# Biases as a 97th row of the weights, one instruction a bank, residual in place, loops written out: a ViT tower kernel

## The chip, the cores and the metric

The kernel runs on one core of one Trainium2 chip. The metric is the device time of one execution in microseconds. Engines are named as in the profile: PE is TensorE (PEld its weight loads), DVE is VectorE, ACT is ScalarE, POOL is GpSimd, SP is SyncE, which here only issues DMAs.

## The reference

Sixteen images of 3 x 64 x 64 are tokenised into 256 tokens of 192 features; then one attention block and one tree-routed feed-forward layer, each with a residual. What the change touches is the attention:

```python
h = tokens(x)                                            # (16, 256, 192)
qkv = layernorm(h) @ W_attn + b_attn                     # 12 heads of 16
scores = q @ k.T / 4, causal; attn = softmax(scores)
h = h + (attn @ v) @ W_proj + b_proj
h = h + fff(layernorm(h), weights_in, weights_out)       # 21 nodes, 11 levels
```

All of it is float32. b_attn and b_proj are not zero.

## The kernel before

There are five hand-written instruction streams, one for each engine, that meet at semaphores. Constants: `B` = 16 images, `S` = 256 tokens (`TT` = 2 tiles of `P` = 128), `D` = 192 features in two halves of `HALF` = 96, `H` = 12 heads, `G` = 3 groups of four heads.

The work has three stages. First the tokens: POOL issues 42 indirect gathers, PE, DVE and ACT turn them into `HT`, the residual stream (128 x 32 tiles x 192, kept in SBUF). Second, sixteen steps, one an image. Third, the second layernorm, the logits, the walk through the tree, and the output.

A step is software-pipelined by hand over four images. `step(b)` on each engine takes the scores and maxima of image b, the last third of the exponentials and the weighted sum of image b-1, the output projection of image b-2, the q, k and v projections of image b+1, and the normalised, transposed tokens of image b+2. Steps 0, 1, 14 and 15 are written out; steps 2 to 13 are a hardware loop (`Fori`) of six trips of two steps on PE, DVE, ACT and POOL. SP's are written out.

What the change and the prediction touch, in the order of PE's stream in a step:

- `qk(b+1, w)`, L1020: for w = 0 (q) and 1 (k) eight float32 matmul instructions of 256 columns (two for each call in the code) into bank `MB`: weights `WA`, moving `XNT`. Then for each w: `first_part` on ACT (L423) rounds the bank plus bias `BQK` to bfloat16 in `PART[0]`; `rest` on DVE (L686) computes bank + bias - `PART[0]` into `RES`; `middle` on ACT (L430) rounds `RES` into `PART[1]`; `low` on POOL (L312) subtracts the two into `PART[2]`. `first_part` and `rest` take two instructions each, since the per-partition bias differs between the two halves of the bank. SP copies the three parts, six 96 x 512 DMAs for q and six for k, into `QS` and `KS` (L251), where six products of parts are stacked on 96 rows.
- `scores(b, u)`, L1047/L1048 and L1052/L1053, u = 0 to 8: scores and mask into two banks; DVE takes their row maxima (L676, L678).
- `minus_max(b, g)` on DVE: two small instructions of 128 x 8, L714 (tensor_scalar) and L716 (scalar_tensor_tensor), write the negated maxima in two bfloat16 parts into `MP`; `max_t(b, g)`, L1073, transposes them on PE; ACT copies them to `MT` (L456); SP copies `MT` into two more rows of `QS` (L258).
- `scores_t(b, v)`, L1090 and L1094: the transposed scores minus maxima; ACT takes the exponentials (L450); POOL cuts them causally (`causal`: L323, L327); `weighted(b, g)`, L1109 and L1112, sums the values.
- `project(b-2)`, L1141; `residual` on DVE (L722) adds bank and `HT` into `H2`; `residual_bias` adds `BP` in place (L728), takes statistics (L732), copies `H2` back into `HT` (L734), aggregates (L736) and copies mean and variance into `MV` (L738).
- `v_proj(b+1)`, L1031, then `values` on DVE: two instructions (L695) add `BV` and write `VA`.
- `on_t(b-1)`, L1132, and `outputs_t` on ACT (L434).
- `xn_t(b+2)`, L1009, which waits for `values` (`v_ok`, same bank); `front` on ACT (L415) copies to `XNT`.

Every engine runs its stream in order. SP's order in a step is the one that the prediction leans on:

```python
sp.wait_ge(st_ps, b.count(SU))       # all scores_t of image b-1
stack(0, 0, QS[1 - par])             # 3 DMAs, waits p0_ok
stack(0, 1, QS[1 - par])             # 2 DMAs, waits p1_ok
maxima(0)                            # 1 DMA, waits mt_ok: needed by scores_t(b, 0)
stack(0, 2, QS[1 - par])             # 1 DMA, waits p2_ok
```

then the same six for k around `maxima(1)` and `maxima(2)`.

## Time and profile before

| | us |
|---|---|
| median of 3 runs | 418.35 |
| the runs | 413.18, 418.35, 418.48 |
| the profiled execution | 411.47 |
| its span, first to last instruction | 409.7 |

| engine | busy us | share of the span |
|---|---|---|
| PE | 341.7 | 83% |
| PEld | 248.1 | 61% |
| DVE | 290.5 | 71% |
| ACT | 217.8 | 53% |
| POOL | 171.7 | 42% |

The mean granted TensorE clock is 0.953 of full speed; through the steps it is full. The tokens take until about 81 us, the sixteen steps until about 365, the rest the tail. Busy time of PE is an upper figure: matmuls are pipelined and their ends are modelled. Idle time in front of an instruction is put down to the event that came last. A matmul's or a weight load's wait on an engine that is nearly always busy is what the time depends on; idle time of DVE, ACT and POOL isn't, by itself. In a timeline row the first number is the start in us from the span's start, the second the time taken, and the bracket the idle time before it with what ended it.

### The profile page before, as it was taken

Reading aid. Unit: us, or ns where it says so; the run is one execution under the profiler, and the core shown is the slowest. Engines: PE = TensorE matmul, PEld = TensorE weight load, DVE = VectorE, ACT = ScalarE, POOL = GpSimd, SP = SyncE. Lnnn points to the kernel's source line nnn. Section 1 sums busy time; section 2 is a strip of 40 time slices with the busy share of each in tenths; the row PEclk is TensorE's granted clock in tenths of the full one; section 3 lists DMA queues with packets and bytes.
Section 4 is the critical chain, followed back from the end, with each engine's and each line's share of the span. In section 5 each row is a group of like instructions: output and inputs, shape, how many; then the busy total and the mean of one; then the engine's idle time right before and its main releaser. Section 6 shows DMA issues by size and latency. Waiting matters only on the chain.

```text
span 409.7 us, 9176 instructions
## 1 busy us (share of the span) xinstructions
PE 341.7 (83%) x2937; PEld 248.1 (61%) x2968; DVE 290.5 (71%) x747; ACT 217.8 (53%) x435; POOL 171.7 (42%) x339
## 2 busy tenths in 40 slices
PE   0779819678898999998999999899999999869745
PEld 0553717446567676675767677576767766547534
DVE  0131564784868888888887898888788768697686
ACT  0304426345565655656565665666566565484753
POOL 5777782223543443354244334424343443344110
PEclk9977978989999999999999999999999999999866
DMA  5962100421303122130312213131230313000008
GB/s 137 193 139 37 22 15 0 116 70 50 107 24 106 49 69 80 37 106 29 97 49 68 87 29 113 32 88 53 64 96 21 116 33 89 1 2 2 2 23 284
DMA packets 33677, 28.03 MB, mean 68 GB/s; under 512 B 7098, under 2 KB 33208, under 8 KB 33656
## 3 DMA queue, kind: packets, MB, share of 16 engines
q1 hardware_dynamic: 32088, 25.41, 22.0%
q0 software_dynamic: 1568, 2.36, 2.7%
q8 instruction: 11, 0.18, 0.2%
q14 instruction: 10, 0.08, 0.1%
HBM read 5.34 MB, written 3.15 MB: 21 GB/s over the span
## 4 chain that ended last, share of the span: by engine, by line
PE 47%; DVE 17%; POOL 10%; issue 9%; ACT 7%; DMA 4%; SPq 4%; another core or an unknown queue 1%; DVEq 0%; ACTq 0%
POOL G L297 7%; PE bank L1020 6%; PE bank L1031 5%; DVE MX L678 4%; PE bank L1109 4%; PE bank L1052 4%; PE bank L1141 4%; SPq L251 4%; DMA QS<-MT 3%; PE bank L1125 3%; PE bank L1094 3%; PE bank L1090 3%; DVE MP L714 2%; PE bank L1073 2%; DVE RES L686 2%
## 5 line engine op out<-in xcount | busy, mean ns | idle before, releaser
L450 ACT ACTIVATE PT<-bank 128x512 f32<-128x512 f32 x144 | 82.3, 595 | 14.6 <-PE bank L1090 10.0
L678 DVE TENSOR_REDUCE MX<-bank 128x2 f32<-128x512 f32 x96 | 64.3, 683 | 8.1 <-PE bank L1053 6.1
L323 POOL TENSOR_TENSOR CARRY<-CARRY 1x1 f32<-1x1 f32 x96 | 17.8, 186 | 122.9 <-ACT PT L450 122.8
L327 POOL TENSOR_SCALAR_AFFINE_SELECT PT<-PT 128x256 f32<-128x256 f32 x144 | 66.2, 472 | 0.0
L1020 PE MATMUL bank<-XNT,WA 96*96 96x256 f32 x256 | 62.8, 389 | 1.9 <-DVE RES L686 1.0
L312 POOL TENSOR_TENSOR PART<-RES,PART 96x512 bf16<-96x512 f32 x32 | 36.9, 1152 | 65.3 <-ACT PART L430 64.6
L676 DVE TENSOR_REDUCE MX<-bank 128x4 f32<-128x512 f32 x48 | 33.0, 688 | 29.6 <-PE bank L1048 15.6
L1020 PEld LDWEIGHTS bank<-XNT,WA 96*96 96x96 f32 x256 | 39.8, 166 | 13.4 <-issue 2.9
L423 ACT ACTIVATE PART<-bank,BQK 96x256 bf16<-96x256 f32 x64 | 26.4, 461 | 23.6 <-PE bank L1020 23.6
L1052 PE MATMUL bank<-KS,QS 96*128 96x256 bf16 x192 | 37.1, 274 | 2.0 <-DVE MX L676 0.9
L297 POOL DMA_INDIRECT G<-x,I x32 | 30.6, 956 | 9.8 <-issue 9.8
L1090 PE MATMUL bank<-QS,KS 98*128 98x256 bf16 x192 | 28.9, 272 | 5.1 <-DMA QS<-MT 4.6
L456 ACT COPY MT<-bank 8x256 bf16<-8x256 bf16 x48 | 17.4, 362 | 29.6 <-PE bank L1073 29.5
L1109 PE MATMUL bank<-PT,VA 128*32 128x256 f32 x384 | 30.7, 390 | 0.0
L686 DVE SCALAR_TENSOR_TENSOR RES<-bank,BQK,PART 96x256 f32<-96x256 f32 x64 | 27.6, 471 | 3.8 <-ACT PART L423 3.8
L430 ACT CAST PART<-RES 96x512 bf16<-96x512 f32 x32 | 19.9, 620 | 17.1 <-DVE RES L686 17.0
L1053 PE MATMUL bank<-MASKQ,IDB 128*128 128x256 bf16 x96 | 26.2, 273 | 0.0
L1031 PE MATMUL bank<-WA,XNT 96*128 96x192 f32 x128 | 24.4, 334 | 1.2 <-DVE RES L686 1.2
L1073 PE MATMUL bank<-IDB,MP 128*8 128x128 bf16 x96 | 13.1, 218 | 13.2 <-DVE MP L716 7.5
L1090 PEld LDWEIGHTS bank<-QS,KS 98*128 98x128 bf16 x192 | 17.7, 97 | 10.2 <-DMA QS<-MT 3.0
L1141 PE MATMUL bank<-WP,ONT 96*128 96x192 f32 x128 | 23.4, 325 | 0.0
L1052 PEld LDWEIGHTS bank<-KS,QS 96*128 96x128 bf16 x192 | 15.5, 98 | 11.9 <-issue 3.6
(133 smaller groups left out, 644.7 us busy)
## 6 DMA issues: line engine op xcount, KB each, us to landing
QS<-PART SPq DMA_DIRECT2D x96, 96.0 KB, 2.9
KS<-PART SPq DMA_DIRECT2D x96, 96.0 KB, 3.0
out<-HT SPq DMA_DIRECT2D x8, 384.0 KB, 2.5
LH<-interp SPq DMA_DIRECT2D x1, 1280.0 KB, 17.0
QS<-MT SPq DMA_DIRECT2D x48, 4.0 KB
G<-x,I POOLq DMA_INDIRECT x42, 5.4
WA<-wa SPq DMA_DIRECT2D x1, 432.0 KB
RH<-Z SPq DMA_DIRECT2D x16, 12.0 KB
```

The source lines that it names most:

```text
L297: pool.indirect_dma_start(G0[:, t, g, :], None, x0, bass.IndirectOffsetOnAxis(ap=I0[:, j:j + 1], axis=0)).then_inc(g0_in[t], 16)
L312: pool.tensor_tensor(PART[2][:, 2 * w:2 * w + 2, :], RES[:, 2 * w:2 * w + 2, :], PART[1][:, 2 * w:2 * w + 2, :], ALU.subtract).then_inc(p2 ...
L327: pool.affine_select(out=e, in_=e, compare_op=ALU.is_ge, fill=0.0, base=0, pattern=[[0, n], [1, P]], channel_multiplier=-1).then_inc(cut_o ...
L450: nc.scalar.activation(PT[:, v, :], BANK[T_BANK[(SU * par + v) % 2]][:, :], ACT.Exp, scale=SCALE).then_inc(exp_ok, 1)
L678: nc.vector.reduce_max(MX[:, 1, HG * g + 2 * r - 2:HG * g + 2 * r], bank[:, :].rearrange("p (h k) -> p h k", h=2), AX.X).then_inc(max_ok, 1)
L686: ins = nc.vector.scalar_tensor_tensor(RES[:, 2 * w + m, :], BANK[MB][0:HALF, m * S:(m + 1) * S], BQK[:, 2 * w + m:2 * w + m + 1], PART[0] ...
L1020: ins = nc.tensor.matmul(BANK[MB][0:HALF, m * S:(m + 1) * S], WA[:, k, (2 * w + m) * HALF:(2 * w + m + 1) * HALF], XNT[:, k, :], start=k = ...
L1031: ins = nc.tensor.matmul(BANK[MB][:, t * D:(t + 1) * D], XNT[:, k, t * P:(t + 1) * P], WA[:, k, 2 * D:3 * D], start=k == 0, stop=k == 1)
L1052: nc.tensor.matmul(bank[:, j * S:(j + 1) * S], QS[par][0:KQ, h, P:S], KS[par][0:KQ, h, :], start=j == 0, stop=False)
L1090: ins = nc.tensor.matmul(bank[:, j * S:(j + 1) * S], KS[par][:, h, 0:P], QS[par][:, h, :], start=j == 0, stop=j == 1)
L1109: nc.tensor.matmul(bank[32 * j:32 * j + 32, c:c + S], VA[par][:, 0, 4 * g + j, :], PT[:, 3 * g + j // 2, (j % 2) * S:(j % 2 + 1) * S], sta ...
L1141: ins = nc.tensor.matmul(BANK[MA][:, t * D:(t + 1) * D], ONT[:, k, t * P:(t + 1) * P], WP[:, k, :], start=k == 0, stop=k == 1)
```

## The change

- `WA`, `WP`, `XNT` and `ONT` get a 97th partition. Row 96 of the weights (its first half only, k = 0) holds the biases, loaded by two more DMAs; row 96 of `XNT` and `ONT` holds ones, written once by two memsets on DVE. The matmuls with k = 0 of `qk`, `v_proj` and `project` contract over 97 rows, those with k = 1 over 96. `BQK`, `BV` and `BP` and their loads go.
- `first_part` becomes one ACT copy of 96 x 512, `rest` one DVE tensor_tensor of 96 x 512.
- `values` moves from DVE (after row_max 7) to ACT (after exp 2, before `outputs_t`), as one copy of 128 x 384.
- `residual` writes its sum straight into `HT`; `H2`'s part in it, the bias add (L728), the copy back (L734) and the copy of mean and variance (L738) go, `bn_aggr` writes `MV` itself. `h2_ok` counts one an image.
- The loops of steps 2 to 13 are written out on PE, DVE, ACT and POOL.

```diff
-        WA = sb("WA", [HALF, 2, 3 * D])
-        WP = sb("WP", [HALF, 2, D])
+        WA = sb("WA", [HB, 2, 3 * D])
+        WP = sb("WP", [HB, 2, D])
...
-                for m in range(2):
-                    ins = nc.scalar.activation(PART[0][:, 2 * w + m, :], BANK[MB][0:HALF, m * S:(m + 1) * S],
-                                               ACT.Identity, bias=BQK[:, 2 * w + m:2 * w + m + 1])
-                ins.then_inc(p0_ok, 1)
+                nc.scalar.copy(PART[0][:, 2 * w:2 * w + 2, :], BANK[MB][0:HALF, :].rearrange("p (m s) -> p m s", m=2)).then_inc(p0_ok, 1)
...
+            def values(b, par):
+                act.wait_ge(v_ps, b.count(1, 1))
+                if not (b.first or b.second):
+                    act.wait_ge(av_ps, (b - 1).count(3))
+                nc.scalar.copy(VA[par][:, :, :, 0:HS], BANK[MB][:, 0:TT * D].rearrange("p (t h d) -> p t h d", t=TT, h=H)).then_inc(v_ok, 1)
...
                 exp(b, par, 2)
+                if has_front:
+                    values(b + 1, 1 - par)
                 if has_back:
                     outputs_t(b - 1)
...
-            with act.Fori(1, B // 2 - 1) as i:
-                step(Image(i, 0), 0, True, True, True, True)
-                step(Image(i, 1), 1, True, True, True, True)
+            for n in range(2, B - 2):
+                step(Image(0, n), n % 2, True, True, True, True)
...
-                for m in range(2):
-                    ins = nc.vector.scalar_tensor_tensor(RES[:, 2 * w + m, :], BANK[MB][0:HALF, m * S:(m + 1) * S],
-                                                         BQK[:, 2 * w + m:2 * w + m + 1], PART[0][:, 2 * w + m, :], ALU.add, ALU.subtract)
-                ins.then_inc(r_ok, 1)
-
-            def values(b, par):
...
+                nc.vector.tensor_tensor(RES[:, 2 * w:2 * w + 2, :], BANK[MB][0:HALF, :].rearrange("p (m s) -> p m s", m=2),
+                                        PART[0][:, 2 * w:2 * w + 2, :], ALU.subtract).then_inc(r_ok, 1)
...
-                hv = HT[:, bass.ds(b.count(TT), TT), :]
-                nc.vector.tensor_tensor(H2[:, :, :], BANK[MA][:, 0:2 * D].rearrange("p (t d) -> p t d", t=2), hv, ALU.add).then_inc(h2_ok, 1)
-
-            def residual_bias(b):
...
+                hv = HT[:, b.count(TT):b.count(TT, TT), :]
+                nc.vector.tensor_tensor(hv, BANK[MA][:, 0:TT * D].rearrange("p (t d) -> p t d", t=TT), hv, ALU.add).then_inc(h2_ok, 1)
+
+            def residual_statistics(b):
+
+                dve.wait_ge(h2_ok, b.count(1, 1))
                 for t in range(TT):
-                    nc.vector.bn_stats(ST2[:, t, :], H2[:, t, :]).then_inc(st2_ok, 1)
-                dve.wait_ge(st2_ok, b.count(2, 2))
-                nc.vector.tensor_scalar(hv, H2[:, :, :], 1.0, None, ALU.mult)
+                    nc.vector.bn_stats(ST2[:, t, :], HT[:, b.count(TT, t), :]).then_inc(st2_ok, 1)
+                dve.wait_ge(st2_ok, b.count(TT, TT))
                 for t in range(TT):
-                    nc.vector.bn_aggr(MV2[:, t, :], ST2[:, t, :]).then_inc(mv2_ok, 1)
-                dve.wait_ge(mv2_ok, b.count(2, 2))
-                nc.vector.tensor_scalar(MV[:, bass.ds(b.count(TT), TT), :], MV2[:, :, :], 1.0, None, ALU.mult).then_inc(mvh_ok, 1)
+                    ins = nc.vector.bn_aggr(MV[:, b.count(TT, t), :], ST2[:, t, :])
+                ins.then_inc(mvh_ok, 1)
...
-                        ins = nc.tensor.matmul(BANK[MB][0:HALF, m * S:(m + 1) * S], WA[:, k, (2 * w + m) * HALF:(2 * w + m + 1) * HALF],
-                                               XNT[:, k, :], start=k == 0, stop=k == 1)
+                        n = HB - k
+                        ins = nc.tensor.matmul(BANK[MB][0:HALF, m * S:(m + 1) * S], WA[0:n, k, (2 * w + m) * HALF:(2 * w + m + 1) * HALF],
+                                               XNT[0:n, k, :], start=k == 0, stop=k == 1)
```

## Rows read from the trace of the kernel before

**Rows 1.** Busy time by windows, steps 7 and 8: PE, PEld, DVE, ACT, POOL, clock

```profile
205.60:223.30 17.70, 17.01 (x159) 12.41 (x159) 14.55 (x38) 10.67 (x22) 7.38 (x18) 1.00 0.23 67
223.30:241.30 18.00, 16.65 (x157) 12.26 (x158) 14.77 (x36) 10.55 (x22) 7.16 (x18) 1.00 0.23 66
```

**Rows 2.** Timeline of step 7: start, time taken, engine, line, [idle before it]

```profile
205.60 1.92 PE L1020 MATMUL bank<-XNT,WA 96*96 96x256 f32 x8
...
210.21 3.13 SPq L251 DMA_DIRECT2D QS<-PART  x5
...
210.82 1.15 POOL L312 TENSOR_TENSOR PART<-RES,PART 96x512 bf16<-96x512 f32 x1 [0.21 <-ACT PART L430]
210.92 1.08 DVE L716 SCALAR_TENSOR_TENSOR MP<-MX,MP 128x8 bf16<-128x8 f32 x1
...
212.06 0.28 PE L1073 MATMUL bank<-IDB,MP 128*8 128x128 bf16 x2
...
213.38 0.65 SPq L258 DMA_DIRECT2D QS<-MT  x1
...
215.83 0.33 PEld L1090 LDWEIGHTS bank<-QS,KS 98*128 98x128 bf16 x4 [0.36 <-DMA QS<-MT]
```

**Rows 3.** Timeline of step 8

```profile
223.19 1.92 PE L1020 MATMUL bank<-XNT,WA 96*96 96x256 f32 x8
...
228.37 1.15 POOL L312 TENSOR_TENSOR PART<-RES,PART 96x512 bf16<-96x512 f32 x1
228.39 1.24 DVE L714 TENSOR_SCALAR MP<-MX 128x8 bf16<-128x8 f32 x1
...
230.40 0.27 PE L1073 MATMUL bank<-IDB,MP 128*8 128x128 bf16 x2 [0.88 <-DVE MP L716]
...
233.91 0.60 PE L1090 MATMUL bank<-QS,KS 98*128 98x256 bf16 x4
```

**Rows 4.** Timeline of step 1, PE: written out, without `project`

```profile
98.77 1.92 PE L1020 MATMUL bank<-XNT,WA 96*96 96x256 f32 x8
...
109.10 0.60 PE L1090 MATMUL bank<-QS,KS 98*128 98x256 bf16 x4 [1.47 <-DMA QS<-MT]
...
116.35 0.84 PE L1020 MATMUL bank<-XNT,WA 96*96 96x256 f32 x3
```

**Rows 5.** Groups by line: xcount | busy us, mean ns | idle before them

```profile
L686 DVE SCALAR_TENSOR_TENSOR RES<-bank,BQK,PART 96x256 f32<-96x256 f32 x64 | 27.6, 471 | 3.8 <-ACT PART L423 3.8
L423 ACT ACTIVATE PART<-bank,BQK 96x256 bf16<-96x256 f32 x64 | 26.4, 461 | 23.6 <-PE bank L1020 23.6
L1141 PE MATMUL bank<-WP,ONT 96*128 96x192 f32 x128 | 23.4, 325 | 0.0
...
L998 PE MATMUL bank<-RH,LH 128*128 128x192 f32 x64 | 12.4, 338 | 0.3 <-ACT LH L399 0.3
...
L434 ACT COPY ONT<-bank 96x512 f32<-96x512 f32 x16 | 9.3, 583 | 21.9 <-PE bank L1132 21.9
...
L728 DVE TENSOR_TENSOR H<-H,BP 128x384 f32<-128x384 f32 x16 | 9.1, 568 | 0.1
L722 DVE TENSOR_TENSOR H<-bank,HT 128x384 f32<-128x384 f32 x16 | 8.7, 545 | 3.0 <-PE bank L1141 3.0
```

**Rows 6.** Timeline of step 6, its end, around `values` and `xn_t`

```profile
202.23 0.62 DVE L695 TENSOR_TENSOR VA<-bank,BV 128x192 f32<-128x192 f32 x2 [0.20 <-PE bank L1031]
...
202.67 0.58 ACT L434 COPY ONT<-bank 96x512 f32<-96x512 f32 x1 [1.53 <-PE bank L1132]
...
203.00 0.61 PE L1009 MATMUL bank<-ID,XN 128*96 128x128 f32 x4
...
204.38 0.27 PE L1073 MATMUL bank<-IDB,MP 128*8 128x128 bf16 x2 [0.32 <-ACT XNT L415]
```

**Rows 7.** Timeline ahead of step 0, images 0 and 1

```profile
75.56 0.87 DVE L686 SCALAR_TENSOR_TENSOR RES<-bank,BQK,PART 96x256 f32<-96x256 f32 x2 [1.94 <-ACT PART L423]
...
79.10 0.61 PE L1009 MATMUL bank<-ID,XN 128*96 128x128 f32 x4 [1.05 <-DVE VA L695]
```

More of the change, by code:

```diff
@@ L14 @@
 HALF = D // 2
+HB = HALF + 1
 F0, F1, F2 = CH, 4 * CH, 16 * CH
@@ L808, in _ @@
             step(Image(0, 1), 1, True, True, True, False)
-            with dve.Fori(1, B // 2 - 1) as i:
-                step(Image(i, 0), 0, True, True, True, True)
-                step(Image(i, 1), 1, True, True, True, True)
+            for n in range(2, B - 2):
+                step(Image(0, n), n % 2, True, True, True, True)
             step(Image(0, B - 2), 0, False, True, True, True)
@@ L1122, in out_t @@
                 else:
-                    pe.wait_ge(h2_ok, (b - 1).count(2, 1))
+                    pe.wait_ge(h2_ok, (b - 1).count(1, 1))
                 for g in range(3):
@@ L1216, in _ @@
             step(Image(0, 1), 1, True, True, True, False)
-            with pe.Fori(1, B // 2 - 1) as i:
-                step(Image(i, 0), 0, True, True, True, True)
-                step(Image(i, 1), 1, True, True, True, True)
+            for n in range(2, B - 2):
+                step(Image(0, n), n % 2, True, True, True, True)
             step(Image(0, B - 2), 0, False, True, True, True)
```

74 lines of the change are left out of this document (30 added, 44 removed).

## The prediction, made before the changed kernel was run

> **What bounds the kernel now.** I read the busy time by windows first, then the waits on PE, then the timeline of three image steps. Two thirds of the span are sixteen image steps of 17.6 to 18.1 us. In the windows of two steps TensorE is busy 17.01 of 17.70 us and 16.65 of 18.00 us [rows 1]. So PE is nearly full, and whatever DVE or ACT saves can only give back PE's idle time, about 0.7 and 1.35 us. The question is which idle time, and what is late next.
>
> Name a step by its image and count from its first L1020 matmul. Odd steps (1, 3, to 13) take about 17.6 us, even ones (2, 4, to 12) about 18.0: step 7 starts at 205.60 and step 8 at 223.19 [rows 2, 3], and the steps alternate like that up to 13. Two places tell them apart.
>
> First, `max_t(b, 0)`, L1073, waits for the two tiny DVE instructions L714 and L716. In step 7 L716 starts at +5.32 and takes 1.08, because POOL's L312 began at +5.22 and runs 1.15; L1073 starts at +6.46 [rows 2]. In step 8 L714 itself comes 0.02 after L312 and takes 1.24; L1073 starts at +7.21, after 0.88 of idle PE [rows 3]. A margin of 0.1 us decides whether one or both are caught.
>
> Second, `scores_t(b, 0)`, L1090, wants the row maxima that SP copies into QS. SP issues five copies of PART first (from +4.61, when `scores_t(b-1, 8)` is over, 3.13 us), and only then L258 at +7.78; the matmul starts at +10.23, its weight load having stood 0.36 for that DMA [rows 2]. Step 8 gets there at +10.72, with PE never idle behind L1073: 3.51 us of matmuls from 230.40 to 233.91 [rows 3]. Step 1 is an experiment made for us: it has no `project`, eight matmuls (23.4 / 16 = 1.46 us) less in just this stretch, it isn't in a loop, and still reaches L1090 at +10.33 after 1.47 idle, and the next step after 17.58 [rows 4, 5]. So +10.2 to +10.3 is a floor that the DMA sets, whatever PE, DVE and ACT do in between.
>
> **The change part by part.**
>
> *Parts (q, k).* L686 goes from two instructions of 0.47 that take 0.87 together [rows 5, 7] to one PSUM-with-SBUF instruction of 96x512. L722, of the same kind with 384 elements, takes 0.54; in proportion 512 would take 0.72, and part of it is fixed. I take 0.68, 0.18 saved; the bounds are 0.54 and 0.72, so 0.15 to 0.33. L423's two of 0.46, some 0.82 together, become one copy like L434, 0.58 [rows 5]: 0.24 saved on ACT. On ACT the saving meets work that waits for PE (exp 6, then the copy after `weighted`), so L430 and L312 don't move against PE. On DVE everything between `rest` and L714 is back to back: L716 moves in step 7 to +5.14, just ahead of L312 at +5.22. In step 8 L714 (+5.20 now) moves to +5.02 and is free; L716 behind it, at +5.22, is either free or caught as in step 7 now. In both cases L1073 is at +6.35 to +6.5.
>
> Can the merged L686 be caught itself? In the rows those caught are L714, L716 and, before step 0, `norm`; no row has L686 beside L312. If it could be, L714 would stay late and even steps as they are (a rival below). The Trainium skill (SBUF — State Buffer, Who interferes with whom) says that a DVE instruction contends with GpSimd only in a 2-port mode or with two SBUF inputs, and that issue order decides. L714 and L716 are of those kinds, so the trace agrees; L686 reads PSUM and one SBUF tensor, so by that rule the sum stays at 411.8 and doesn't become 414.8.
>
> What is late next: in odd steps L1090 already stands at the floor, so a freed L716 only makes it wait longer for the DMA: 0. In even steps L1090 goes from +10.72 to the floor: 0.49 (0 if L714 stays caught; 0.88 if there were no floor, with L1073 at +6.33, its 0.88 of idle gone, and 3.51 behind it).
>
> *Values.* `values` leaves DVE (two of 192 elements, 0.62 together) for ACT, after exp 2, in front of `outputs_t` [rows 6]. ACT has 1.53 us idle there [rows 6]. One copy of 128x384 costs at most L434's 0.58 and by its size some 0.5; I take 0.48. It starts with the end of `v_proj` as L695 did, so v_ok comes 0.14 earlier (0.04 to 0.2). `xn_t`, L1009, waits for it, then `front` on ACT, then `max_t(b, 2)`, which stood 0.32 for that XNT [rows 6]. `outputs_t` could start at 202.67 and the copy ends at 202.71, overlapping: 0. I take 0.15 in each of steps 1 to 13; the bounds are 0 and the whole 0.32. The DVE time freed isn't on the path: row_max 8 waits for PE.
>
> *Residual.* L728 (0.57 [rows 5]) and the two copies L734 and L738 go, over 1 us of DVE at the end of each step. What follows them on DVE is `norm(b + 2)`, wanted only by `xn_t` late in the next step, and row_max 0, which waits for PE's scores. So they lie under PE's `qk` and are worth 0 in the loop. h2_ok is signalled by the same instruction, L722, in place now at the same size. If something hung there it would be at most 0.1.
>
> *The 97th row.* The same number of matmuls and columns, 97 rows instead of 96 in half of them. The f32 matmul of 192 columns takes 0.325 with 96 rows (L1141) and 0.338 with 128 (L998) [rows 5]. If all of that 0.013 were row cost, a step's 16 of this kind would pay at most 0.2, for 32 rows more, and one row nothing; I take 0. The memsets of ones, the loads of three bias tiles less and of two rows more lie under the gathers that POOL issues at the start: 0.
>
> *Unrolling.* Step 1, outside the loop, is as long as step 7 inside it [rows 2, 4]. So the loop's register work costs PE nothing. I take 0, bounds 0.1 a step either way.
>
> *Before step 1.* For image 0 the chain is `qk`, L423, L686, twice in series: 2 x (0.24 + 0.18) = 0.84. From the second L686's end, 76.43, to `xn_t` of image 1 at 79.10 it is 2.67 us, in which PE does `v_proj` and DVE `norm` and then `values` [rows 7]: with `values` on ACT it is 1.5 of matmuls like `project`'s, 0.5 and some 0.2 of handing over, 2.2: 0.45. Together 1.3, and 0.5 if DVE's other work ahead of step 0 doesn't come forward with it. Step 0 has one rest and one values on its chain: 0.3.
>
> *Behind step 13.* Step 14 has no `xn_t`, and in the chain of waits ACT's table loads and the exchange between PE and ACT set the tail, with none of the removed instructions on it: 0.
>
> Sum: 6 even steps x (0.49 + 0.15) = 3.8; 7 odd x 0.15 = 1.05; 1.3; 0.3. Total 6.5 us: the span 409.7 becomes 403.2, the profiled execution's 411.47 becomes 405.0. The median shown is 418.35, 6.9 above that execution, with runs from 413.18; taking the same 6.5 from it gives 411.8.
>
> **The rivals.**
>
> *No floor.* If the maxima's DMA came earlier, L1090 would sit at +9.84 in all 13 steps: 0.38 each, 5 us more, 406.9. Against it stands step 1.
>
> *L714 stays caught.* If even steps keep L1073 at +7.2 (L312 moves with the copy in front of it, or the new L686 is no shorter), only 1.3 + 0.3 + 13 x 0.15 = 3.5 is left: 414.8. For it speaks that the margin is 0.02 to 0.18 us; against it that L312 follows PE through ACT and DVE alone moved.
>
> *Nothing but the prologue.* If v_ok isn't what holds `xn_t`, and the above holds too: 1.6 saved, 416.8.
>
> *Slower: the instruction stream.* Unrolled, each engine's stream is read once, not six trips of the same two steps. If a step then had to wait for its instructions, PE, which is nearly full, would pass it on. It decides from 0.5 us a step (14 steps x 0.5 = 7); at 1.1 us a step it is 418.35 - 6.5 + 15.4 = 427.2, slower by over 2%. Against it: steps 0, 1 and 14 are straight code already and show nothing of it.
>
> **How the numbers follow.** The floor case 0.55, no floor 0.12, L714 caught 0.15, prologue alone 0.08, slower 0.05, others 0.05. The predicted time is the first's, 411.8; its own range is 406 to 416, mostly the scatter of the runs (413.18 to 418.48 for one kernel). The range of 8 in 10 takes in the other two below and above: 404 to 418. 2% of 418.35, about what a measurement of this kernel tells from no change, is 8.4 us, so faster means below 410.0: a third of the first case (0.19), nearly all of the second (0.11), little of the third (0.02): 0.32. Slower 0.05, same 0.63.
>
> **What would show it.** Right: L1073 at +6.3 to +6.5 in all steps; L1090 at +10.2 to +10.3 in even steps too, with a wait for the QS DMA in all thirteen, longer in odd ones; steps of 17.4 all alike; L686 one of 0.67; v_ok's copy on ACT 0.48; `xn_t` of image 1 near 77.8; DVE's maxima in front of it as long as now. DVE's busy time falls by at least 16 x (4 x 0.47 - 2 x 0.68 + 0.62 + 0.57) = 27 us, and most of that buys nothing. Wrong: L1090 before +10.0; L1073 at +7 in any step; PE standing with nothing to wait for, at places that move with the code; ACT's exp 3 later against L1009 than now.

## The result, and where the time is

The changed kernel takes 423.28 us (median of 4 executions, 419.01 to 425.42) against 416.15 for the kernel before it: ratio 1.02, 95% interval 1.0145 to 1.0255. Some executions fall in a slower state at a lower granted clock, so the ratios leave those out while the medians do not, and a ratio is not exactly the quotient of two medians. The changed kernel is slower, by about 7 us, clear of the noise and outside the predicted range; whether it is slower by more than 2% the interval leaves open. Its profiled execution took 419.01 us with a span of 417.2, 7.5 above the span of before.

Cut both spans at the first matmul of each stage. From the first `qk` to step 0 the changed kernel is faster, 11.68 to 10.48 us. Step 0 goes from 18.29 to 17.84. Steps 1 to 13 together go from 231.47 to 236.46: 5.0 lost. Steps 14 and 15, up to the start of the last transposed scores, lose 0.9. The first `qk` comes 0.8 later and the stage behind step 15 takes 2.5 longer. Sum: -1.2 - 0.45 + 5.0 + 0.9 + 0.8 + 2.5 = 7.5.

Two windows of the changed kernel, steps 7 and 8 (columns as in [rows 1]):

```profile
206.46:225.24 18.78, 16.70 (x158) 12.32 (x158) 11.91 (x29) 10.60 (x22) 7.22 (x17) 1.00 0.28 64
225.24:243.40 18.16, 16.71 (x159) 12.32 (x158) 11.92 (x29) 10.60 (x22) 7.22 (x17) 1.00 0.30 67
```

DVE's busy time has fallen by nearly 3 us a step, TensorE's has not moved, and the steps are 18.2 and 18.8 us where the windows of before were 17.7 and 18.0 [rows 1]. The DMA share (the column before the last) is 0.28 and 0.30 where it was 0.23, for the same copies. Step 8 of the changed kernel in its timeline:

```profile
229.86 3.13 SPq L248 DMA_DIRECT2D QS<-PART  x5
...
230.37 0.17 DVE L705 TENSOR_SCALAR MP<-MX 128x8 bf16<-128x8 f32 x1
...
230.47 1.15 POOL L309 TENSOR_TENSOR PART<-RES,PART 96x512 bf16<-96x512 f32 x1
230.57 1.15 DVE L707 SCALAR_TENSOR_TENSOR MP<-MX,MP 128x8 bf16<-128x8 f32 x1
...
231.77 0.27 PE L1057 MATMUL bank<-IDB,MP 128*8 128x128 bf16 x2 [0.18 <-DVE MP L707]
...
233.04 0.65 SPq L255 DMA_DIRECT2D QS<-MT  x1
...
236.29 0.60 PE L1074 MATMUL bank<-QS,KS 98*128 98x256 bf16 x4 [0.84 <-DMA QS<-MT]
```

On DVE the small instructions stand where they were forecast, if for another reason than the forecast's (below): the first one (L705, once L714) slips in ahead of POOL's and takes 0.17 instead of 1.24, and the transpose of the maxima (L1057, once L1073) starts at +6.53 instead of +7.21 [rows 3]. SP issues the copy of the maxima at +7.80, as before (+7.78 [rows 2]). But the matmul that needs it (L1074, once L1090) starts at +11.05, 3.25 us behind the issue, with TensorE idle for 0.84. In step 7 of before it started 2.45 behind the issue [rows 2]. The waits of TensorE in 134 to 352 us (what waits, for what: us, count, longest), first the changed kernel, then the kernel before:

```profile
PE bank L1074 <- DMA QS<-MT: 11.1, 15, 1.5
```

```profile
PEld bank L1090 <- DMA QS<-MT: 2.1, 6, 0.4
PE bank L1090 <- DMA QS<-MT: 0.8, 2, 0.5
```

So the transfer itself is slower. The DMA sections of the two profile pages (queue: packets, MB, share of 16 engines' time; last number of an issue row: us to landing) show it for all copies. Kernel before:

```profile
q1 hardware_dynamic: 32088, 25.41, 22.0%
...
QS<-PART SPq DMA_DIRECT2D x96, 96.0 KB, 2.9
KS<-PART SPq DMA_DIRECT2D x96, 96.0 KB, 3.0
out<-HT SPq DMA_DIRECT2D x8, 384.0 KB, 2.5
```

Changed kernel:

```profile
q1 hardware_dynamic: 31692, 25.21, 26.0%
q0 software_dynamic: 1568, 2.36, 2.8%
q8 instruction: 24, 0.39, 0.5%
...
QS<-PART SPq DMA_DIRECT2D x96, 96.0 KB, 3.2
KS<-PART SPq DMA_DIRECT2D x96, 96.0 KB, 3.4
out<-HT SPq DMA_DIRECT2D x8, 384.0 KB, 3.1
```

1% fewer packets take 4 points more of the engines' time. In time a packet: 0.220 x 16 x 409.7 / 32088 = 45 ns before, 0.260 x 16 x 417.2 / 31692 = 55 ns after. That is a mean over everything on the queue, loads and small packets too; the packets of 1024 bytes in steps 3 to 12, which are the PART copies alone, take 54.2 ns on average before and 68.5 after, 26% more. The instruction fetches (q8) have doubled, but at half a per cent they are no load.

**What the diff does not say.** It takes three tiles away, `BQK` (32 bytes a partition), `BV` and `BP` (768 each), and every tile allocated behind them moves down by 1568 bytes. In the compiled kernels `PART0` goes from byte 64000 of a partition to 62432, `QS0` from 74240 to 72672, `HT` from 34304 to 32736. Before, each of them began on a multiple of 512. After, each begins 480 past one, which is 224 past a multiple of 256. The copies move rows of 1024 bytes between these tiles.

**Theory A**: the loss is the address of these tiles. **Theory B**: it is the instruction stream of the written-out loops. **Theory C**: it is the work moved between engines (values on ACT, one instruction a bank).

### The profile page after: what moved, and what is told of

It is laid out like the page before. It is cut to its first block, busy times and chain, and to the rows that moved or that the text cites. A ratio compares the mean times of both kernels' runs of the same rounds, so it can differ in the third digit from the quotient of the medians.

```text
span 417.2 us, 8253 instructions
## 1 busy us (share of the span) xinstructions
PE 337.7 (81%) x2937; PEld 249.1 (60%) x2968; DVE 250.3 (60%) x637; ACT 217.6 (52%) x419; POOL 170.9 (41%) x339
## 3 DMA queue, kind: packets, MB, share of 16 engines
q1 hardware_dynamic: 31692, 25.21, 26.0%
q0 software_dynamic: 1568, 2.36, 2.8%
HBM read 5.14 MB, written 3.15 MB: 20 GB/s over the span
## 4 chain that ended last, share of the span: by engine, by line
PE 43%; SPq 13%; DMA 12%; DVE 9%; POOL 9%; issue 7%; ACT 4%; DVEq 0%; another core or an unknown queue 0%; ACTq 0%
SPq L248 13%; DMA QS<-MT 11%; POOL G L294 7%; PE bank L1003 7%; PE bank L1015 4%; PE bank L1093 4%; PE bank L1074 4%; PE bank L1036 4%; PE bank L1078 3%; DVE MX L680 3%; PE bank L1109 2%; POOL G L290 2%; PE bank L1057 2%; PE bank L1096 2%; PE bank L1031 2%
## 5 line engine op out<-in xcount | busy, mean ns | idle before, releaser
L680 DVE TENSOR_REDUCE MX<-bank 128x2 f32<-128x512 f32 x96 | 65.5, 684 | 25.1 <-PE bank L1037 23.5
L320 POOL TENSOR_TENSOR CARRY<-CARRY 1x1 f32<-1x1 f32 x96 | 17.7, 184 | 136.1 <-ACT PT L449 136.1
L1003 PE MATMUL bank<-XNT,WA 97*96 97x256 f32 (+1 forms) x256 | 63.3, 390 | 1.3 <-ACT XNT L411 0.8
L678 DVE TENSOR_REDUCE MX<-bank 128x4 f32<-128x512 f32 x48 | 33.0, 688 | 51.9 <-remote 36.8
L1003 PEld LDWEIGHTS bank<-XNT,WA 97*96 97x96 f32 (+1 forms) x256 | 40.0, 166 | 13.1 <-issue 2.3
L1074 PE MATMUL bank<-QS,KS 98*128 98x256 bf16 x192 | 28.8, 271 | 18.3 <-DMA QS<-MT 18.3
L1074 PEld LDWEIGHTS bank<-QS,KS 98*128 98x128 bf16 x192 | 17.1, 96 | 25.5 <-issue 19.8
L418 ACT CAST PART<-bank 96x512 bf16<-96x512 f32 x32 | 18.4, 575 | 22.7 <-PE bank L1003 22.7
L423 ACT CAST PART<-RES 96x512 bf16<-96x512 f32 x32 | 19.8, 617 | 16.9 <-DVE RES L687 16.9
L1037 PE MATMUL bank<-MASKQ,IDB 128*128 128x256 bf16 x96 | 26.2, 273 | 0.0
L1015 PE MATMUL bank<-WA,XNT 96*128 96x192 f32 (+1 forms) x128 | 24.5, 333 | 0.7 <-DVE RES L687 0.7
L1126 PE MATMUL bank<-WP,ONT 96*128 96x192 f32 (+1 forms) x128 | 24.0, 330 | 0.0
L687 DVE TENSOR_TENSOR RES<-bank,PART 96x512 f32<-96x512 f32 x32 | 21.6, 676 | 3.3 <-ACT PART L418 3.3
L707 DVE SCALAR_TENSOR_TENSOR MP<-MX,MP 128x8 bf16<-128x8 f32 x48 | 21.7, 452 | 1.6
```

Source lines behind the costliest of these rows:

```text
L678: nc.vector.reduce_max(MX[:, 0, HG * g:HG * (g + 1)], bank[:, :].rearrange("p (h k) -> p h k", h=4), AX.X).then_inc(max_ok, 1)
L680: nc.vector.reduce_max(MX[:, 1, HG * g + 2 * r - 2:HG * g + 2 * r], bank[:, :].rearrange("p (h k) -> p h k", h=2), AX.X).then_inc(max_ok, 1)
L1003: ins = nc.tensor.matmul(BANK[MB][0:HALF, m * S:(m + 1) * S], WA[0:n, k, (2 * w + m) * HALF:(2 * w + m + 1) * HALF], XNT[0:n, k, :], start ...
L1015: ins = nc.tensor.matmul(BANK[MB][:, t * D:(t + 1) * D], XNT[0:n, k, t * P:(t + 1) * P], WA[0:n, k, 2 * D:3 * D], start=k == 0, stop=k == 1)
L1074: ins = nc.tensor.matmul(bank[:, j * S:(j + 1) * S], KS[par][:, h, 0:P], QS[par][:, h, :], start=j == 0, stop=j == 1)
```

## The experiments

All times are medians of executions beside executions of the kernel before on the same chip; "(one)" is a single execution, and d_part has too few executions for a ratio. For the kernels with 445 in brackets every kernel of that occasion, the one before included, took some 28 us longer ahead of the steps, so I compare ratios there, and above all the mean length of steps 1 to 13 in the profiled execution, which for one kernel come again within 0.1 us. In b_shift480 and d_qk step 1 ran at a granted clock of 0.91 and took 19.81 and 19.71 us; without it their means are 18.35 and 18.20. Where ratios and steps disagree, the difference lies outside the steps, where the granted clock varies from execution to execution; for the loop the steps decide. Ratios from different occasions differ by about 1% for kernels with like steps, so only ratios of one occasion are compared closely. "ns a packet" is worked out as above, from the q1 row and the span, over the whole queue.

| kernel | PART, QS/KS past a multiple of 256 | us | ratio, 95% interval | mean of steps 1 to 13 | ns a packet |
|---|---|---|---|---|---|
| before | 0, 0 | 416 (445) | 1 | 17.81 | 45 |
| after | 224, 224 | 423.28 | 1.02, 1.0145 to 1.0255 | 18.19 | 55 |
| a_pad32 | 0, 0 | 412.05 | 0.9865, 0.9743 to 0.9986 | 17.63 | 45 |
| a_pad32_again | 0, 0 | 411.14 | 0.9844, 0.9782 to 0.9907 | 17.71 | 45 |
| a_pad288 | 0, 0 | 409.15 (one) | | 17.55 | 46 |
| a_pad64 | 32, 32 | 423.80 (one) | | 18.33 | 53 |
| a_pad96 | 64, 64 | 419.63 | 1.0106, 1.0001 to 1.021 | 18.14 | 50 |
| b_shift480 | 224, 224 | 425.41 | 1.0222, 1.0127 to 1.0316 | 18.46 | 56 |
| b_unrolled | 0, 0 | 416.40 | 1.0002, 0.9942 to 1.0062 | 17.71 | 45 |
| d_part | 224, 0 | 439.00 (445.19) | | 17.58 | 47 |
| d_qk | 0, 224 | 449.89 (445.19) | 1.0177, 1.0098 to 1.0256 | 18.32 | 52 |
| c_order | 0, 0 | 447.97 (445.19) | 0.9999, 0.9917 to 1.0081 | 17.73 | |
| e_values_dve | 0, 0 | 442.70 (445.19) | 0.9965, 0.9914 to 1.0016 | 17.67 | |
| c_order2 | 0, 0 | 401.07 | 0.9651, 0.9609 to 0.9692 | 17.10 | 45 |
| c_order2_again | 0, 0 | 430.55 (445.81) | 0.9682, 0.9635 to 0.9729 | 17.11 | |
| after_order2 | 224, 224 | 408.23 | 0.9846, 0.9784 to 0.9908 | 17.14 | 52 |
| after_order2_again | 224, 224 | 439.24 (445.81) | 0.9851, 0.9791 to 0.991 | 17.22 | |
| b_order2 | 0, 0 | 409.44 | 0.9873, 0.9812 to 0.9934 | 17.25 | |
| o2_values_dve | 0, 0 | 407.46 | 0.9801, 0.9734 to 0.9869 | 17.19 | |

### The address, both ways round

a_pad32 is the changed kernel with an unused tile of 32 bytes where the three bias tiles were; it puts all later tiles back on multiples of 512:

```diff
         BFB = sb("BFB", [P, D])
+        PAD = sb("PAD", [P, 8])
```

> The changed kernel with one unused SBUF tile of 32 bytes a partition in front of what the dropped bias tiles stood in front of. It puts PART, QS, KS, HT and all behind them back to multiples of 512 bytes, where they stood in the kernel before; in the changed kernel they start 480 bytes past such a multiple (PART0 went from byte 64000 to 62432, QS0 from 74240 to 72672). Theory A, addresses: the copies of PART into QS and KS (1 KB packets) are slower only because of where the tiles start. Then the share of the DMA queue falls from 26% to about 22%, the maxima's DMA lands 2.4 us after its issue and not 3.1, L1074 of a step starts at +10.2 to +10.3, the steps are 17.3 to 17.4 us and the span about 409.7 - 6.5 = 403, ratio to before about 0.985. Theory B, instruction stream: the written-out loops (39 instruction fetches where there were 21) disturb the DMA queues; then nothing changes against the changed kernel: 26%, steps of 18.2, ratio 1.02. Theory C, engines: ACT and DVE write or read in other places and slow the DMAs down; also no change.

b_shift480 is the kernel before with `[P, 120]` at the same place, and nothing of the change.

> The kernel before, with an unused SBUF tile of 480 bytes a partition behind BFB, so that PART, QS, KS start 480 bytes past a multiple of 512, as in the changed kernel; nothing else is different. Theory A: the kernel becomes slower by what the floor rises, 0.7 to 0.9 us in each of 13 steps less what even steps have in hand (0.5): span 409.7 + 13 x 0.75 - 6 x 0.5 = about 416.5, ratio 1.015 to 1.02, DMA share 26%. Theories B and C: no change, ratio 1.00.

Eight unused floats turn 1.02 into 0.985, and 120 unused floats turn the kernel before into one that is as slow as the changed one. The page of b_shift480 has the changed kernel's DMA rows:

```profile
q1 hardware_dynamic: 32088, 25.41, 26.6%
...
QS<-PART SPq DMA_DIRECT2D x96, 96.0 KB, 3.2
KS<-PART SPq DMA_DIRECT2D x96, 96.0 KB, 3.4
```

and that of a_pad32 those of before:

```profile
q1 hardware_dynamic: 31692, 25.21, 21.7%
...
QS<-PART SPq DMA_DIRECT2D x96, 96.0 KB, 2.9
KS<-PART SPq DMA_DIRECT2D x96, 96.0 KB, 3.0
```

This is theory A, shown in both directions. Theory C falls with a_pad32, which has all of the moved work and is faster than before. Theory B falls with a_pad32 too, whose loops are written out, and had its own run, the kernel before with its loops written out:

```diff
-            with act.Fori(1, B // 2 - 1) as i:
-                step(Image(i, 0), 0, True, True, True, True)
-                step(Image(i, 1), 1, True, True, True, True)
+            for n in range(2, B - 2):
+                step(Image(0, n), n % 2, True, True, True, True)
```

> The kernel before with the four loops of steps 2 to 13 written out and nothing else; all tiles stay where they are. Theory B: slower, 1.015 to 1.02, with L1090 late behind the maxima's DMA. Theory A, and the prediction's step on unrolling: PE intervals as before; even steps may become like odd ones (L714 ahead of L312), which would be 6 x 0.48 = 2.9 us less, ratio 0.993 to 1.00.

No difference in time that the interval can show (1.0002, 0.9942 to 1.0062); steps 1 to 13 of the profiled execution are 1.2 us shorter in sum. Within the loop two things change. First, the alternation of 17.6 and 18.05 us is gone, and with it the late maxima of the even steps. Step 8 of b_unrolled, which starts at 226.83 (L712 and L714 here are L714 and L716 of the kernel before, L1070 is L1073):

```profile
231.95 0.17 DVE L712 TENSOR_SCALAR MP<-MX 128x8 bf16<-128x8 f32 x1
232.06 1.15 POOL L312 TENSOR_TENSOR PART<-RES,PART 96x512 bf16<-96x512 f32 x1
232.15 1.15 DVE L714 SCALAR_TENSOR_TENSOR MP<-MX,MP 128x8 bf16<-128x8 f32 x1
...
233.36 0.28 PE L1070 MATMUL bank<-IDB,MP 128*8 128x128 bf16 x2 [0.19 <-DVE MP L714]
```

These are +5.12, +5.23, +5.32 and +6.53 of the step, the same places and durations as in the changed kernel, and so it is in every step from 2 to 13. What freed the first small instruction is therefore the writing out of the loops, with nothing of the merged instructions. Second, steps 7 and 11 are 18.49 and 18.11, because SP takes 4.18 us for the five copies that it elsewhere issues in 3.13:

```profile
212.95 4.18 SPq L251 DMA_DIRECT2D QS<-PART  x5
217.17 0.65 SPq L258 DMA_DIRECT2D QS<-MT  x1
```

The changed kernel, a_pad32, a_pad64, a_pad96, a_pad288, d_part, d_qk and e_values_dve, all with written-out loops and SP's old order, have late copies in steps 7 and 11 too; the kernel before and b_shift480, with hardware loops, have none. SP's own program is written out in both. What holds SP there I have not tested.

### Which offset, and which side of the copy

a_pad96 (`[P, 24]`, 64 past a multiple of 512), a_pad64 (`[P, 16]`, 32 past) and a_pad288 (`[P, 72]`, 256 past) are a_pad32 with another size of the pad.

> The changed kernel with an unused tile of 96 bytes: PART, QS and KS start 64 bytes past a multiple of 512. Theory A has two forms. A64: a start on a multiple of 64 bytes is enough, then as with 32 bytes, ratio 0.985. A256: a packet is cut at every 256 bytes; by the Trainium skill (DMA: Bandwidth & Descriptors, How a descriptor splits into AXI transactions) a 1024-byte packet is 32 beats from an aligned start, 39 from 224 past a multiple of 256 (five pieces, as in the changed kernel) and 34 from 64 past one; so an estimate by that page is packets 6% longer than aligned where the changed kernel's are 22% longer (its mean packet of 1024 bytes went up 26% by the traces): landing of the maxima about 2.6, ratio about 0.99. Theories B and C: 1.02.

> The changed kernel with 64 bytes of padding, so that PART, QS, KS start 32 bytes past a multiple of 512. If a copy's cost follows the 256-byte pieces that it is cut into, 33 units of 32 bytes against 32: q1 share about 22.4% and steps of 17.7 us. If any start off a multiple of 64 bytes costs as 480 did: share near 26%, steps 18.2. If what counts is that the packet touches one more 256-byte piece, as at 64 bytes: share 23.8%, steps 18.2.

> The changed kernel with 288 bytes of padding, so that PART, QS, KS start 256 bytes past a multiple of 512. If the boundary that counts is 256 bytes: share 21.7%, steps 17.6 us, as aligned. If it is 512: share 23.8% or more, steps of about 18.2.

256 past a multiple of 512 costs nothing (17.55 us a step, one execution), so by these runs the period is 256 bytes (or a part of it), not 512. Every offset inside it that I tried costs: 32 bytes 53 ns a packet (one execution), 64 bytes 50, 224 bytes 55, against 45. For the 1024-byte packets of steps 3 to 12 alone it is 66.9, 62.5 and 68.5, against 54.5. The steps pay 0.4 to 0.7 us for each of them, the first two as much as the third. The Trainium skill (DMA: Bandwidth & Descriptors, How a descriptor splits into AXI transactions) says that a descriptor is cut at 256-byte boundaries and that the unused bytes ahead of an unaligned start are fetched too, in beats of 32 bytes. An estimate by that page for a row of 1024 bytes is 32 beats aligned, 39 at an offset of 224, 34 at 64 and 33 at 32: 22%, 6% and 3% more. Nothing at 256 is as it says. At 224 the whole queue's mean gives its 22%, the 1024-byte packets alone 26%; at 64 they give 12% and 15%, at 32 18% and 23%. So the count of beats does not tell the time, and the match at 224 is no proof of it: the next two runs show that the side that is read, of which the page speaks, has the smaller part. What the rest is, no run here shows.

d_part and d_qk keep a_pad32's places for everything but one side of the copies, and put the rest back behind it:

```diff
+        PADA = sb("PADA", [P, 120])
         PART = [sb(f"PART{i}", [HALF, 4, S], bf16) for i in range(PARTS)]
+        PADB = sb("PADB", [P, 8])
```

> The changed kernel with every tile back at its aligned place (412.05 us), but only the three PART tiles, the source of the PART to QS and KS copies, start 480 bytes past a multiple of 512 (120 floats of padding ahead of them, 8 behind). If the reading side of a copy sets its cost: share of the queue q1 near 26%, the scores group 0 of a step waits for the DMA of the maxima (L1074 in the changed kernel) near 11 us in all, 423 us. If the writing side sets it: share 21.7%, 412 us. If either side alone costs part: between, about 23.9% and 417 us.

> The same base (412.05 us), but only the QS and KS tiles, the destination of the copies, start 480 bytes past a multiple of 512; PART stays aligned. If the writing side sets the cost: q1 near 26%, 423 us. If the reading side sets it: 21.7%, 412 us. If each costs part: about 23.9%, 417 us. If the two sides are handled one behind the other the two runs' excesses over 21.7% add up to the 4.3 points of the changed kernel; if they overlap and the slower sets it, each alone shows the whole 4.3.

Moving the tiles that are read costs 2 ns a packet (47 against 45) and no step time (17.58). Moving the tiles that are written costs 7 (52) and the whole of the loop's loss (18.32, or 18.20 without step 1, against 18.19 in the changed kernel). The sum, 9, is near the 10 of the changed kernel, so the two sides add. The 1024-byte packets of steps 3 to 12 say the same: 59.0 and 65.0 against 54.5, and 68.5 with both. The side that matters more is the one written. The waits of d_qk in steps 3 to 12 (L1077 are the transposed scores in both):

```profile
PE bank L1077 <- DMA QS<-MT: 8.8, 10, 1.4
```

and of d_part:

```profile
PE bank L1077 <- DMA QS<-MT: 2.4, 8, 0.6
```

### The floor: the maxima's place in SP's order

How can slower packets cost 0.5 us a step, when the DMA engines are 70% idle? The answer is the floor of the prediction. From the timelines of steps 3 to 12:

| kernel | maxima's copy issued | first transposed score | us between |
|---|---|---|---|
| before, odd steps | +7.78 | +10.11 to +10.28 | 2.3 to 2.5 |
| after | +7.79 (8 of 10 steps) | +10.6 to +11.1 | 2.8 to 3.3 |
| b_shift480 | +7.79, +7.91 | +10.8 to +11.05 | 3.0 to 3.2 |
| a_pad32 | +7.79 (8 of 10) | +10.05 to +10.6 | 2.3 to 2.8 |
| d_part | +7.79 (8 of 10) | +10.06 to +10.5 | 2.3 to 2.7 |
| d_qk | +7.79 (8 of 10) | +10.8 to +11.1 | 3.0 to 3.3 |
| c_order2 | +7.23 | +10.06 | TensorE busy |
| after_order2 | +7.23 | +10.06 | TensorE busy |

The copy of 4 KB is queued behind five of 96 KB. Its own eight packets are mostly moved 1.4 us behind its issue, before and after alike, but the semaphore of the copy gets its last event only at 2.2 to 2.45 us before and 2.65 to 3.15 after (steps 3 to 12), near the landing of the fifth PART copy, at 2.1 to 2.9 and 2.6 to 3.1. So it is released when the large copies in front are nearly through. c_order (built on a_pad32, as c_order2 is) takes two of them from in front of it:

```diff
                 stack(0, 0, QS[1 - par])
-                stack(0, 1, QS[1 - par])
                 maxima(0)
+                stack(0, 1, QS[1 - par])
                 stack(0, 2, QS[1 - par])
```

> The changed kernel with aligned tiles (412.05 us) and one edit: the copy of the maxima of group 0 is issued behind three PART copies in place of five. The floor that the prediction named: maxima ready at about +6.9 of a step, the copy issued at +7.8 behind the fifth PART copy, the first transposed score at +10.3 to +10.5. If the floor is the place in SP's order, the issue moves to +7.0, the transposed scores start up to 0.5 earlier in the steps where they wait for the copy (5.3 us of waits over 14 steps in the aligned kernel): 407 to 409 us. If the landing time itself or TensorE's own work sets it, no change: 412. If the PART copies that now come 0.8 later are late for the next step's scores: 413 to 416.

The transposed scores of group 0 came to +10.06 in every step from 2 on, with no wait, and nothing was gained (0.9999, steps 17.73): the next copy of maxima, group 1, now stood behind more PART copies, and TensorE waited for that one. Its waits for the copies of maxima in steps 1 to 13 went up, from 6.3 us in a_pad32 to 12.2, and steps 14 and 15 took 37.8 us against 35.7. One step of c_order:

```profile
206.50 0.60 PE L1075 MATMUL bank<-QS,KS 98*128 98x256 bf16 x4
...
212.44 0.60 PE L1075 MATMUL bank<-QS,KS 98*128 98x256 bf16 x4 [0.74 <-DMA QS<-MT]
```

c_order2 moves that one as well:

```diff
                 stack(1, 0, KS[1 - par])
-                stack(1, 1, KS[1 - par])
                 maxima(1)
+                stack(1, 1, KS[1 - par])
                 stack(1, 2, KS[1 - par])
```

> As c_order (the copy of the maxima of group 0 issued behind three PART copies instead of five), and the copy of the maxima of group 1 issued behind the three KS copies of PART0 instead of five. c_order freed the transposed scores of group 0 (+10.06 in every step, no wait) and lost it again in those of group 1 (0.74 us of wait for the maxima's copy in one step, steps 17.6 to 18.3). If the two copies' places in SP's order are all that holds the step above TensorE's own work (16.7 us a step), the steps fall to 17.2 us and the kernel to 0.4 times 14, 5.6 us, under a_pad32: ratio to before about 0.975. If the copies behind them come too late for KS, or the third group's copy holds the step: 17.6, ratio 0.987.

401.07 us, ratio 0.9651, every step from 3 on 17.17 us: the fastest kernel of this study, ahead of both. The copies are issued at +7.23 and +12.50 of the step that starts at 182.10:

```profile
186.72 1.85 SPq L249 DMA_DIRECT2D QS<-PART  x3
189.33 0.66 SPq L256 DMA_DIRECT2D QS<-MT  x1
190.03 1.85 SPq L249 DMA_DIRECT2D QS<-PART  x3
191.93 2.62 SPq L249 DMA_DIRECT2D KS<-PART  x3
194.60 0.66 SPq L256 DMA_DIRECT2D QS<-MT  x1
195.30 1.86 SPq L249 DMA_DIRECT2D KS<-PART  x3
```

after_order2 is the same order in the changed kernel as it stands, unaligned; b_order2 in the kernel before (b_unrolled), with nothing of the change.

> The changed kernel, tiles unaligned as it has them, with the copies of the maxima of groups 0 and 1 issued behind three PART copies instead of five. Aligned, that order gave steps of 17.17 us (c_order2). If the loss of the changed kernel goes only through the wait for the maxima's copy in TensorE's queue, its slack now covers the slower packets in part: the copy is issued 0.8 earlier and lands 0.6 later, steps of 17.2 to 17.3, ratio to before about 0.975. If the slower PART copies also hold the next step's scores or the other groups: steps of 17.6 to 18.2, ratio 0.99 to 1.02.

> The kernel before with its loops written out (416.4 us, ratio 1.0002) and the new order of SP's copies, none of the change in it. If the order alone makes the gain of c_order2: ratio 0.966, steps 17.2. If the change's freed DVE and ACT time matters as well (in the kernel before, DVE's maxima of groups 0 and 1 hold TensorE up to 0.88 us in every other step, and nothing hides it once the copy is early): steps between 17.4 and 17.7, ratio 0.98 to 0.995.

With the floor gone the unaligned kernel has steps of 17.17 as well: the slower packets are still there (52 ns), and nobody in the loop waits for them. The semaphore's last event now comes 1.75 to 2.2 us behind the issue at +7.23, by +9.5, and the matmul wants it at +10.06. So the loop's loss goes through this one wait. The kernel before has 17.30 a step in the new order, a gain of 0.5, and the change is then worth 0.13 a step more (17.30 to 17.17). In the old order the same comparison, b_unrolled against the aligned changed kernel, gives 17.71 against 17.63 and 17.71: next to nothing as long as the DMA set the step.

after_order2 and c_order2, equal in the loop, are still 7 us apart in the medians. I ran both again, side by side.

> c_order2 once more, beside after_order2 on the same chip. If its 401.07 belongs to the kernel: 400 to 403 again, ratio 0.965. If the clock outside the loop was a draw of that call: anywhere from 401 to 408, and after_order2 with it, the two within 2 us (the end of the output, 1 us, and step 0).

> after_order2 once more. If the unaligned tiles cost some 7 us outside the loop as well (loads, step 0, output): 408 again, ratio 0.985, beside 401 for c_order2. If it is the clock: within 2 us of c_order2 in this call, whichever level both have.

The ratios came again, 0.968 and 0.985, so the gap is not one occasion's. Of the 9.8 us between the two spans, the first `qk` has 2.0, step 0 4.6 (21.82 against 17.22), steps 1 to 13 1.4, steps 14 and 15 0.7, and the end 1.05. The end is the output of `HT`, from the start of the last eight matmuls 7.1 against 6.1 us, at granted clocks of 0.74 and 0.78, as in the first pair (7.0 and 6.1), with `out<-HT` landing in 3.1 against 2.7. `HT` starts at 480 in the one and on a multiple of 512 in the other, and d_qk and d_part, with `HT` aligned and other tiles not, land it in 2.7; so I put it down to the address of `HT`, which I did not move alone. The rest I can only describe: where step 0 takes 20 us, the granted clock is 0.83 in it instead of 1.00 and TensorE waits some 1.4 us for a copy of KS; but an aligned kernel, o2_values_dve, has just such a step 0 too (20.20). How far address, clock and start hang together there stays open.

### The values

e_values_dve and o2_values_dve are a_pad32 and c_order2 with the values copied out by DVE again, as one instruction between row maxima 7 and 8:

```diff
-                nc.scalar.copy(VA[par][:, :, :, 0:HS], BANK[MB][:, 0:TT * D].rearrange("p (t h d) -> p t h d", t=TT, h=H)).then_inc(v_ok, 1)
+                nc.vector.tensor_copy(VA[par][:, :, :, 0:HS], BANK[MB][:, 0:TT * D].rearrange("p (t h d) -> p t h d", t=TT, h=H)).then_inc(v_ok, 1)
```

> The changed kernel with aligned tiles (412.05 us), but the values are copied out by DVE, at the place in its order where the kernel before had them, as one instruction. The prediction gave ACT's earlier copy 0.15 us a step, 13 steps: 2.0 us. If that term is right: 414.0 us. If TensorE or the copy of the maxima sets the step either way: 412. If DVE's queue was what held the weighted sums more than forecast: 415 or more.

> c_order2 (ratio 0.9651, steps of 17.17 us) with the values copied out by DVE at the place of the kernel before, as one instruction. If the term of 0.15 us a step for ACT's copy is real: steps of 17.3, ratio 0.970. If it is nothing, because the group 2 maxima wait for XNT or for DVE either way: 17.17, ratio 0.965. If DVE's queue is what holds the step now (TensorE waits 7.3 us for MP): 17.4 or more, ratio 0.975.

In the clean loop of o2_values_dve a step is 17.25 instead of 17.17: 0.08 us, with TensorE waiting for XNT again, 3.6 us over eleven steps:

```profile
PE bank L1058 <- ACT XNT L412: 3.6, 11, 0.3
```

The medians, 407.46 against 401.07, say more, but it lies outside the loop (the first `qk` comes 2.8 us later, step 0 takes 3.0 more, the stage behind step 15 2.2 more). e_values_dve and a_pad32 were not measured side by side, so their ratios (0.9965 against 0.9865 and 0.9844) decide nothing between them; their steps are 17.67 against 17.63 and 17.71. Ahead of step 0 the values have a price of their own: from the first `qk` to step 0 it is 10.75 us in both kernels with DVE's copy and 10.48 with ACT's.

> The same kernel as a_pad32 (the changed kernel with 32 bytes of padding behind BFB), for a narrower interval: its ratio was 0.9865 [0.9743, 0.9986]. If the tiles' addresses are the whole of the loss, the steps 3 to 13 take 17.6 us each whatever the chip, the q1 share by time is that of the kernel before, and the ratio lies between 0.98 and 0.99; if the first run was a lucky draw of the clock, within 0.5% of 1.

The second run of a_pad32 narrows its interval: 0.9844, 0.9782 to 0.9907. The address alone is worth 0.985 against 1.02.

## The prediction, step by step

**TensorE nearly full.** Right: 16.7 of 18.2 us, and 16.55 of 17.17 in c_order2.

**The floor.** This is the step that failed. It was right that a DMA sets the first transposed score, right where, and right that the freed L714 and L716 would only lengthen the wait for it. Wrong was "a floor that the DMA sets, whatever PE, DVE and ACT do in between", at +10.2 to +10.3: the floor was read from one kernel and taken as a constant of the step, though it is an issue time plus the landing of the copies in front and its own, and the landing depends on where the tiles lie. The part's other sentence, that three bias tiles less are worth 0, looked at the loads and not at what their absence does to the addresses. The first transposed score moved to about +11.05, 0.8 more than odd steps had and 0.3 more than even ones: 7.8 us in sum over steps 1 to 13, against 2.8 gained behind L1074 (0.22 a step). That is the 5.0 lost. No rival had it. The rival that ended on the slower side, the instruction stream, had the sign by another mechanism; the ratio measured for it alone is 1.0002.

**Even steps gain 0.49, odd ones 0.** With aligned tiles the first half is nearly right and the second wrong. In a_pad32 the first transposed score of the even steps comes at +10.37 on average instead of +10.73, 0.36 gained, but that of the odd ones at +10.57 instead of +10.23, 0.34 lost: its copy, issued at +7.79, takes 2.3 to 2.8 where odd steps before had 2.3 to 2.5, and in steps 7 and 11 it is issued late. Over the thirteen the sum is 0.25 us worse than before. b_unrolled has both effects without the rest of the change, so the even steps' gain and the odd steps' loss both came with the written-out loops.

**L686 merged, 0.68; L423 merged, 0.58; L714 free.** The durations are right, 0.676 and 0.575, and L1073 is at +6.53 (forecast 6.35 to 6.5). But the reason given for that is wrong, and that it came true is luck. "On DVE everything between `rest` and L714 is back to back", so that the 0.18 saved in L686 reaches L714, does not hold: the first row maximum behind it starts 0.18 earlier than in b_unrolled (+3.61, +3.79), the second, whose scores' matmul L1037 ends at +4.36, starts at +4.40 against +4.39. Step 8 of the changed kernel (from 225.24; L680 and L1037 are L678 and L1053 of the kernel before):

```profile
228.25 0.68 DVE L687 TENSOR_TENSOR RES<-bank,PART 96x512 f32<-96x512 f32 x1
228.85 1.48 DVE L680 TENSOR_REDUCE MX<-bank 128x2 f32<-128x512 f32 x2
...
229.33 0.27 PE L1037 MATMUL bank<-MASKQ,IDB 128*128 128x256 bf16 x1
```

and of b_unrolled (from 226.83):

```profile
229.84 0.86 DVE L684 SCALAR_TENSOR_TENSOR RES<-bank,BQK,PART 96x256 f32<-96x256 f32 x2
230.62 1.29 DVE L676 TENSOR_REDUCE MX<-bank 128x2 f32<-128x512 f32 x2
```

The two maxima begin 0.18 earlier and end at +5.09 and +5.08. The first small instruction is at +5.12 in both, and it is free because the loops are written out, the part of the change that was priced at 0. The merged rows:

```profile
L418 ACT CAST PART<-bank 96x512 bf16<-96x512 f32 x32 | 18.4, 575 | 22.7 <-PE bank L1003 22.7
...
L687 DVE TENSOR_TENSOR RES<-bank,PART 96x512 f32<-96x512 f32 x32 | 21.6, 676 | 3.3 <-ACT PART L418 3.3
```

They answer to L423 and L686 in [rows 5]. L716 stays caught by POOL (1.15), as in step 7 before; the rival that L714 stays caught did not come about, though no run has the merged instructions inside the loops.

**Values, 0.48 on ACT, 0.15 a step.** The duration is right, the price half: 0.08 in the new order (o2_values_dve), and 0.04 or less in the old one (e_values_dve). L1057 of group 2 waits no longer for XNT but 0.32 for DVE's MP, which the prediction did not look at:

```profile
222.10 0.48 ACT L429 COPY VA<-bank 128x384 f32<-128x384 f32 x1 [1.10 <-PE bank L1015]
222.54 0.58 ACT L433 COPY ONT<-bank 96x512 f32<-96x512 f32 x1
...
222.72 0.61 PE L991 MATMUL bank<-ID,XN 128*96 128x128 f32 x4
...
224.09 0.27 PE L1057 MATMUL bank<-IDB,MP 128*8 128x128 bf16 x2 [0.32 <-DVE MP L707]
```

From the first transposed scores of step 8 to the start of step 9 it is 7.11 us (236.29 to 243.40), against 7.33 before (233.91 [rows 3] to 241.24): 0.22, of which the values are 0.08 at most. The same stretch, as a mean over steps 1 to 13, is 7.34 before, 7.25 in b_unrolled and 7.15 in a_pad32, so about 0.09 comes with the written-out loops; the few hundredths left I have not split.

**Residual, the 97th row, unrolling: 0.** The row: `project` takes 1.47 for eight matmuls against 1.46, so 0. Unrolling: 0 in time as far as b_unrolled can tell (1.2 us in the sum of the steps), though not in shape, as said under L714. Residual: DVE's busy time fell by 40 us (290.5 to 250.3, forecast at least 27), and I did not test it alone.

**Before step 1: 1.3 and 0.3.** 11.68 to 10.48 from the first `qk` to step 0 is 1.2; the values on ACT have 0.27 of it (forecast 0.45) by the kernels with 10.75, and the other 0.93 (forecast 0.84 for the merged instructions) goes to the rest of the change. Step 0 is 0.45 shorter at nearly the same clock (0.91, 0.90). The span shows only 0.4 of the 1.2, since the first `qk` came 0.8 later; in one kernel, a_pad32, it comes at 69.57 or at 72.11, with the granted clock between 20 and 40 us at about 0.97 or at 0.66.

**Behind step 13: 0.** The stage behind step 15 is 2.5 longer. Up to the last transposes of the second layernorm it loses 1.7 (19.94 to 21.62), at a granted clock of 0.89 instead of 0.98; a_pad32_again, aligned, takes 21.56 there too, at 0.90. From there to the last eight matmuls it wins 0.7 (18.56 to 17.83, clock 0.59 and 0.69). From their start to the end it loses 1.5 (5.6 to 7.1, clock 0.81 and 0.74). At like clocks c_order2 and after_order2 differ there by 1.0, with `out<-HT` landing in 2.7 and 3.1: that part I put down to the slower output of `HT`, the same oversight again.

The sum, 411.8, is what the changed kernel takes when its tiles lie where they lay: 412.05 and 411.14. That agreement is luck for the most part. The loop gave less (1.3 to 2.2 of the 4.85 forecast for steps 1 to 13). The 6.5 were taken from a median of three, 418.35, where later medians of the kernel before are 416.15 to 416.8, and the spans of the profiled executions are 410.6 and 408.9 against 409.7, not 403.2.

## What to carry to other kernels

When an edit adds or drops an SBUF tile, list where the tiles behind it come to lie, above all those that a DMA writes: here the copies of 1024-byte rows took 15% to 26% longer a packet with both sides off a multiple of 256 bytes, and a pad of 32 bytes gave back 3.5%. A floor read from a trace is a sum (issue time, what is queued ahead, landing), and each term has to be asked what the edit does to it. When several edits go in together, one of them can do what another is credited with: writing out the loops alone shows which freed the maxima. If a small transfer that the busiest engine waits for is queued behind large ones that nobody wants yet, move it forward, and then look at the next such transfer, since the first move alone gained nothing.
